# A layernorm's transposes take turns on the PSUM banks of the score maxima, not on those of heads and sums

## The chip, the cores and the metric

The kernel runs on one core of a Trainium2 chip. The metric is the device time of one execution in microseconds, from the first to the last instruction and what the launch adds around them; lower is better.

## What is computed

Eight sequences of 512 rows of 512 floats go through two layers: a cross attention to 77 rows of context (here "L", for L0) and then a block with self attention, a second cross attention (here "cross") and an MLP. Each begins with a layernorm. Cut to what matters:

```python
def cross_attention(x, context):                  # once as "L", once as "cross"
    h = layernorm(x)                              # "L" also scales and shifts it
    q = h @ Wq + bq                               # 16 heads of 32
    k, v = split(layernorm(context) @ Wkv + bkv)  # 77 keys, prepared ahead
    p = softmax(q @ k.T / sqrt(32))               # 512 x 77 for each head
    return x + (p @ v) @ Wp + bp
x = cross_attention(x, ctx)        # "L"
x = x + gate_a * self_attention(modulate(layernorm(x)))
x = cross_attention(x, ctx)        # "cross"
x = x + gate_m * mlp(modulate(layernorm(x)))
```

## The kernel before

Everything is float32 split into a high and a low part, so a product is three matmuls (`product`, line 396). Each engine has one instruction stream, written out in a fixed order by Python generators that `braid` interleaves step by step; between engines only semaphores order the work. A matmul's output goes to one of eight PSUM banks. A `Turns` ring hands its banks out in order, and `take` gives back what the bank's last user must have done before it may be written; TensorE (PE) waits for that.

A context attention works through 32 steps n: a batch b (of 8) and a group g of four heads (of 4). In a step PE has, interleaved:

- `attend`: four matmuls of scores by key (line 1318), banks 0 and 1, each read by ScalarE's exponential (line 1400). After the first of them `values` runs for the step before: the heads' sums over the values (line 1332, "heads") and the sums of the exponentials (line 1339, "sums"). These take the ring `pairs`, banks 6 and 7.
- `maxima` of step n + 3: for each of four tiles of rows, scores for the row maximum (line 396 on `key_diagonals`, M0 to M3 below), and VectorE's reduce (line 1217, `negated_max`). `max_rows` transposes the maxima (line 1304, R below), then ScalarE and VectorE write them in two parts (lines 1387 and 1225), and DMAs put them into the query stack. M0 to M3 and R take the ring `max_banks`, banks 2 and 3, in the order M0, R of the step before, M1, M2, M3.
- query products of a step further ahead and projections of the batch before (both line 396).

`Norm` normalises the rows of a coming batch and turns them: four groups of four transposes (line 354, T0 to T3 below), each into one bank. In "L" ScalarE modulates it into a float tile (line 377, which frees the bank) and splits it (379; VectorE 329). In "cross" ScalarE reads the bank for the high part (381) and VectorE reads it again for the low part (329), which frees it. The turns of batches 0 and 1 have a ring of their own. Those of batches 2 to 7 come in one step each, so there are six such places in each of the two attentions; a place begins with T0, in a step with g = 3, and ends in the next step, called ' below (M0', R', M1'). In "L" each is followed by a product of the modulation that belongs to the preparation (line 765), which takes a bank of `pairs` too:

```python
self.scores, self.max_banks, self.pairs = k.ring(0, 1), k.ring(2, 3), k.ring(6, 7)
```

```python
bk, before = self.ring(b).take((self, i), self.wide(i) if self.mods else self.lo(i))
if before:
    pe.wait_ge(*before)
for t in range(NT):
    turn = e.transpose(...)
```

Of the kernel before, what the change touches and what calls it, by code (L numbers as in the profile page):

```python
# [55 lines left out]
class Done:  # L56


    def __init__(self, sem, base, by):
        self.sem, self.base, self.by = sem, base, by  # L60
# [859 lines left out]
class CrossAttention:  # L920
# [5 lines left out]
    def __init__(self, k, w, name, layer, tail, first_banks, first_turns, x_in, x_ready, x_out, eps, mods, mods_ready, wq, bq, wp, bp, at):  # L926
        self.k, self.w, self.name, self.layer, self.tail = k, w, name, layer, tail
        self.x_in, self.x_out, self.wq, self.bq, self.wp, self.bp, self.at = x_in, x_out, wq, bq, wp, bp, at
        self.products, self.first_products = k.ring(4, 5), k.ring(*first_banks)
        self.scores, self.max_banks, self.pairs = k.ring(0, 1), k.ring(2, 3), k.ring(6, 7)  # L930
        self.norm = Norm(k, x_in, x_ready, eps, mods, mods_ready, 1, (k.ring(*first_turns), self.pairs), 2)
        n, c = LAST, k.count
        self.bias_loaded = c("dma_projection_bias", 1, 16)
        self.key_ones, self.diagonal_zeros = c("vector_key_ones", 2), c("pool_diagonal_zeros", 2)
        self.k_loaded, self.v_loaded = k.slots("key_stack", 2, B, 3), k.slots("values", 2, B)
        self.d_loaded = k.slots("key_diagonals", 2, B, 2 * GH)
        self.q_product = c("tensor_queries", n)
        self.q_hi, self.q_lo = c("scalar_queries_hi", n), c("vector_queries_lo", n)
        self.q_stored, self.q_stacked = k.slots("query_store", 2, n), k.slots("query_stack", 4, n, 3)
        self.smax, self.negmax = c("tensor_scores_for_max", n * NT), c("vector_negated_maxima", n * NT)  # L940
        self.rows_turned = c("tensor_turned_maxima", n)
        self.row_hi, self.row_lo = c("scalar_max_row_hi", n), c("vector_max_row_lo", n)
        self.rows_put = k.slots("max_rows", 4, n, 2)
        self.score, self.exp = c("tensor_scores_by_key", n * GH), c("scalar_exponentials", n * GH)
        self.av, self.summed = c("tensor_value_sums", n), c("tensor_exponential_sums", n)
        self.heads_copied, self.heads_hi = c("scalar_heads_float32", n), c("scalar_heads_hi", n)
        self.sums_turned, self.inverted = c("vector_sums_turned", n), c("vector_reciprocals", n)
        self.spread, self.normalised = c("vector_reciprocals_spread", n), c("vector_normalised_heads", n)
        self.heads_lo = c("vector_heads_lo", n)
        self.x_loaded, self.x_stored = k.slots("context_x_rows", 2, B), k.slots("context_x_out", 2, B)  # L950
        self.based, self.projected = c("pool_residual_bases", B * NT), c("tensor_projections", B * NT)
        self.added = c("vector_residuals", B * NT)
        self.place()
# [1425 lines left out]
```

## Time and profile before

| | |
|---|---|
| median of 3 runs | 2582.3 us (2569.95 to 2584.04) |
| profiled execution | 2574.66 us, span 2572.9 us |
| PE busy | 2401.8 us, 93% of the span |
| VectorE (DVE) busy | 1380.0 us, 54% |
| ScalarE (ACT) busy | 1026.1 us, 40% |
| mean granted TensorE clock | 0.972 |

The profiled execution is the one whose rows are read below. Its span is the time from its first to its last instruction; 1.8 us lie around it. The granted clock is a share of full speed: 1.00 is 2.4 GHz, 0.50 is 1.2 GHz.

### The profile page before, as it was taken

How to read it: one execution, taken by the hardware profiler on the slowest of the kernel's cores; microseconds unless marked ns; L12 is line 12 of the kernel's file. 1: busy time of each engine (PE TensorE's matmuls, PEld its weight loads, DVE VectorE, ACT ScalarE, POOL GpSimd, SP SyncE). 2: the span in 40 equal slices, each digit the busy share in tenths (PEclk: the TensorE clock that was granted, in tenths of full speed). 3: DMA queues.
4: the chain of work that ended last, by engine and by line, in shares of the span. 5: the costliest groups of instructions: out<-in, count | busy, mean ns of one | idle time of the engine just before them, and what ended most of it. 6: DMA issues, size and time to landing. Idle time of an engine off the chain costs nothing. (4 is left out here: it accounts for less than half of the span.)

```text
span 2572.9 us, 32327 instructions
## 1 busy us (share of the span) xinstructions
PE 2401.8 (93%) x12048; PEld 1683.8 (65%) x12048; DVE 1380.0 (54%) x2463; ACT 1026.1 (40%) x1831; POOL 588.1 (23%) x325
## 2 busy tenths in 40 slices
PE   6889999999979899999998789999899999999998
PEld 5656666678867344444444456766588888888887
DVE  4566666644546877776777456676743222222221
ACT  3454444423322455555554334444442322233231
POOL 2101111110000466665665411111211011101100
PEclk9899999999989899999999899999999999999999
DMA  6687777554564446565453568786531101110110
GB/s 205 193 216 229 206 216 200 173 197 176 180 212 147 104 112 153 132 153 130 116 144 90 146 157 221 200 230 184 166 114 58 58 1 58 58 58 1 58 42 17
DMA packets 261275, 354.19 MB, mean 138 GB/s; under 512 B 60979, under 2 KB 109195, under 8 KB 261118
## 3 DMA queue, kind: packets, MB, share of 16 engines
q1 hardware_dynamic: 259950, 348.27, 47.9%
q0 software_dynamic: 1168, 3.85, 0.4%
q8 instruction: 96, 1.57, 0.3%
q14 instruction: 61, 0.50, 0.1%
HBM read 233.78 MB, written 116.69 MB: 136 GB/s over the span
## 5 line engine op out<-in xcount | busy, mean ns | idle before, releaser
L1813 DVE TENSOR_REDUCE negated_max<-banks 128x1 f32<-128x512 f32 x512 | 331.8, 675 | 140.7 <-PE banks L1878 140.4
L1977 ACT ACTIVATE self_exponentials<-banks 128x512 f32<-128x512 f32 x512 | 286.3, 594 | 283.8 <-PE banks L1899 133.0
L1779 POOL TENSOR_TENSOR self_exponentials<-self_exponentials,self_exponentials 128x2048 f32<-128x2048 f32 x64 | 303.1, 4736 | 217.0 <-ACT self_exponentials L1977 217.0
L2177 PE MATMUL banks<-mlp_w_down_hi,out_parts 128*128 128x512 f32 x1024 | 333.8, 389 | 0.1
L337 POOL TENSOR_SCALAR norm_rstd<-norm_mean_var 128x4 f32<-128x4 f32 x32 | 8.0, 249 | 1336.3 <-DVE norm_mean_var L316 1336.3
L2134 DVE TENSOR_TENSOR out_parts<-wide,out_parts 128x512 fp32r<-128x512 f32 x128 | 93.1, 727 | 371.6 <-ACT out_parts L2206 371.6
L1899 PE MATMUL banks<-self_query_stack,self_key_stack 98*128 98x512 f32 x512 | 236.4, 463 | 26.3 <-ACT self_exponentials L1977 23.5
L2196 ACT ACTIVATE wide<-banks,bias_columns 128x512 f32<-128x512 f32 x128 | 88.3, 690 | 426.0 <-PE banks L396 425.9
L1899 PEld LDWEIGHTS banks<-self_query_stack,self_key_stack 98*128 98x128 f32 x512 | 98.1, 192 | 212.6 <-ACT self_exponentials L1977 173.3
L2177 PEld LDWEIGHTS banks<-mlp_w_down_hi,out_parts 128*128 128x128 f32 x1024 | 192.2, 188 | 40.4 <-DVE cross_last_x_rows L1261 0.5
L1878 PE MATMUL banks<-self_key_stack,self_query_stack 96*128 96x512 f32 x512 | 207.4, 408 | 2.3 <-DVE negated_max L1813 2.1
L2177 PE MATMUL banks<-mlp_w_down_lo,out_parts 128*128 128x512 f32 x512 | 199.2, 389 | 0.0
L1217 DVE TENSOR_REDUCE negated_max<-banks 128x4 f32<-128x308 f32 x256 | 121.0, 473 | 100.4 <-PE banks L396 96.7
L1921 PE MATMUL banks<-self_exponentials,self_values 128*32 128x512 f32 x1024 | 140.4, 621 | 0.7 <-ACT self_exponentials L1977 0.7
L312 DVE BATCH_NORM_STATS2 norm_stats<-norm_x 128x6 f32<-128x512 f32 x128 | 84.6, 671 | 67.0 <-DMA norm_x<-x 66.7
L1400 ACT ACTIVATE cross_exponentials<-banks 77x512 f32<-77x512 f32 x128 | 75.3, 591 | 106.6 <-PE banks L1318 106.6
L377 ACT ACTIVATE wide<-banks,modulation_columns 128x512 f32<-128x512 f32 x96 | 74.5, 776 | 104.7 <-PE banks L354 97.3
L396 PE MATMUL banks<-x_hi,w_qkv_hi 128*128 128x512 f32 x256 | 101.2, 395 | 16.0 <-DVE out_parts L1531 15.1
L1590 ACT ACTIVATE out_parts<-banks,bias_columns 128x512 fp32r<-128x512 f32 x64 | 44.1, 689 | 179.6 <-PE banks L396 144.1
L1400 ACT ACTIVATE L_exponentials<-banks 77x512 f32<-77x512 f32 x128 | 75.3, 591 | 87.9 <-PE banks L1318 87.7
L2177 PEld LDWEIGHTS banks<-mlp_w_down_lo,out_parts 128*128 128x128 f32 x512 | 96.1, 188 | 20.0
L1878 PEld LDWEIGHTS banks<-self_key_stack,self_query_stack 96*128 96x128 f32 x512 | 99.8, 195 | 14.2 <-DVE negated_max L1813 5.6
(208 smaller groups left out, 5253.4 us busy)
## 6 DMA issues: line engine op xcount, KB each, us to landing
L_query_stack<-q_parts_L SPq DMA_DIRECT2D x96, 256.0 KB, 4.8
norm_x<-x SPq DMA_DIRECT2D x24, 1024.0 KB, 7.5
self_query_stack<-q_parts_self SPq DMA_DIRECT2D x96, 256.0 KB, 4.0
self_key_stack<-k_parts_self SPq DMA_DIRECT2D x96, 256.0 KB, 6.3
cross_query_stack<-q_parts_cross SPq DMA_DIRECT2D x96, 256.0 KB, 5.0
x_rows<-x SPq DMA_DIRECT2D x23, 1024.0 KB, 6.7
x<-x_rows SPq DMA_DIRECT2D x22, 1024.0 KB, 5.0
q_parts_L<-out_parts SPq DMA_DIRECT2D x32, 512.0 KB, 4.6
```

What stands on the lines that cost most here:

```text
L396: mm = e.matmul(out_ap, l, r, start=i == 0, stop=i == len(terms) - 1)
L1217: e.tensor_reduce(k.nm[n % 2][:, t:GH * NT:NT], k.bank[:, bk, 0:GH * S].rearrange("p (h k) -> p h k", k=S), AX_X, ALU.max, negate=True).th ...
L1400: e.activation(self.p[:, i % self.HEADS_KEPT, :], k.bank[0:S, self.scores.of["score", i], :], ACT.Exp, scale=SCALE).then_inc(self.exp.sem, 1)
L1779: e.tensor_tensor(self.p[kt - 1][:], self.p[kt - 1][:], self.p[kt][:], ALU.add).then_inc(self.paired.sem, 1)
L1813: e.tensor_reduce(k.nm[n % 2][:, h * NT + t:h * NT + t + 1], k.bank[:, self.max_banks.of["max", i], :], AX_X, ALU.max, negate=True).then_i ...
L1878: e.matmul(k.bank[:, bk, :], self.q[n % 4][0:ST, h, t * P:(t + 1) * P], self.keys[n % 4][0:ST, h, :], start=True, stop=True).then_inc(self ...
L1899: e.matmul(k.bank[:, bk, :], self.keys[n % 4][0:ST_MAX, h, kt * P:(kt + 1) * P], self.q[n % 4][0:ST_MAX, h, :], start=True, stop=True).the ...
L1921: mm = e.matmul(k.bank[h * HD:(h + 1) * HD, bk, :], self.v[n % 3][:, kt, h * HD:(h + 1) * HD], self.p[kt][:, h, :], start=kt == 0, stop=kt ...
L1977: e.activation(self.p[kt][:, h, :], k.bank[:, self.scores.of["score", i], :], ACT.Exp, scale=SCALE).then_inc(self.exp.sem, 1)
L2134: e.tensor_tensor(h[:, 1, :], k.wides[k.wide_turns.of["up", i]][:], raw(h[:, 0, :]), ALU.subtract).then_inc(self.lo.sem, 1)
L2177: mm = e.matmul(bank, l, w, start=j == 0 and q == 0, stop=j == JC - 1 and q == 2)
L2196: e.activation(k.wides[w][:], k.bank[:, self.banks.of["up", i], :], ACT.Gelu_apprx_tanh, bias=k.bias_cols[:, col:col + 1]).then_inc(self.w ...
```

## The change

From batch 2 on, T0 to T3 of both context attentions take turns on banks 2 and 3 (`max_banks`) in place of banks 6 and 7 (`pairs`). No instruction is added, removed or moved on any engine. Only the banks change, and with them what PE waits for before it writes one.

```diff
         self.scores, self.max_banks, self.pairs = k.ring(0, 1), k.ring(2, 3), k.ring(6, 7)
-        self.norm = Norm(k, x_in, x_ready, eps, mods, mods_ready, 1, (k.ring(*first_turns), self.pairs), 2)
+        self.norm = Norm(k, x_in, x_ready, eps, mods, mods_ready, 1, (k.ring(*first_turns), self.max_banks), 2)
```

PE's stream in "cross", at the end of a place of a batch from 3 on. The first rows are T2 and T3, then come the first score of the next step, M0', R', the heads and the sums. In brackets stand the semaphores that a row waits for; `vector_norm_lo` is VectorE's low part, the last reader of a turned bank.

```order
+L354 MATMUL banks<-identity,norm_x 128x128 [waits vector_negated_maxima]
+L354 MATMUL banks<-identity,norm_x 128x128 x3
 L354 MATMUL banks<-identity,norm_x 128x128 [waits vector_norm_lo]
 L354 MATMUL banks<-identity,norm_x 128x128 x3
-L354 MATMUL banks<-identity,norm_x 128x128 [waits vector_norm_lo]
-L354 MATMUL banks<-identity,norm_x 128x128 x3
 L1318 MATMUL banks<-cross_query_stack_167,cross_key_stack_172 77x512 [waits dma_key_stack1,scalar_exponentials,dma_max_rows0,dma_query_stack0]
-L396 MATMUL banks<-cross_key_diagonals_174,out_parts_65 128x308 [waits vector_negated_maxima]
+L396 MATMUL banks<-cross_key_diagonals_174,out_parts_65 128x308 [waits vector_norm_lo]
 L396 MATMUL banks<-cross_key_diagonals_174,out_parts_65 128x308 x2
-L1304 MATMUL banks<-identity,negated_max_83 16x128 [waits vector_negated_maxima]
-L1332 MATMUL banks<-cross_exponentials,cross_values_175 32x512 [waits scalar_exponentials,vector_norm_lo]
```

The wait for T2's reader moved from the heads (line 1332) to M0', and the wait for T3's reader, which the sums (line 1339) had, moved to R' (line 1304), ahead of the heads and the sums. T2 itself now waits for the reduce of M3.

PE's stream in "L", the same place's end; `scalar_norm_float32` is ScalarE's modulation, the reader that frees a turned bank there.

```order
-L1304 MATMUL banks<-identity,negated_max_83 16x128 [waits vector_negated_maxima]
-L1332 MATMUL banks<-L_exponentials,L_values_130 32x512 [waits scalar_exponentials,scalar_norm_float32]
+L1304 MATMUL banks<-identity,negated_max_83 16x128 [waits scalar_norm_float32]
+L1332 MATMUL banks<-L_exponentials,L_values_130 32x512 [waits scalar_exponentials,scalar_heads_float32]
 L1332 MATMUL banks<-L_exponentials,L_values_130 32x512 x3
-L1339 MATMUL banks<-L_exponentials,ones 32x512 [waits scalar_norm_float32]
+L1339 MATMUL banks<-L_exponentials,ones 32x512 [waits vector_sums_turned]
 L1339 MATMUL banks<-L_exponentials,ones 32x512 x3
```

Here too the waits for ScalarE moved from the heads and sums to the two matmul groups ahead of them.

PE's stream in "cross" at the first of the six places (batch 2), where no projection stands between T0 and T3.

```order
-L354 MATMUL banks<-identity,norm_x 128x128 [waits scalar_heads_float32,vector_normed_rows]
+L354 MATMUL banks<-identity,norm_x 128x128 [waits vector_negated_maxima,vector_normed_rows]
 L354 MATMUL banks<-identity,norm_x 128x128 x3
 L1318 MATMUL banks<-cross_query_stack_170,cross_key_stack_171 77x512 [waits scalar_exponentials]
 L396 MATMUL banks<-cross_key_diagonals_174,out_parts_64 128x308 [waits vector_negated_maxima]
 L396 MATMUL banks<-cross_key_diagonals_174,out_parts_64 128x308 x2
-L354 MATMUL banks<-identity,norm_x 128x128 [waits vector_sums_turned]
-L354 MATMUL banks<-identity,norm_x 128x128 x3
 L354 MATMUL banks<-identity,norm_x 128x128 [waits vector_norm_lo]
```

T0 now waits for the reduce of M1, and T1 for T0's own reader, where it waited for the sums' transpose.

## Rows read from the trace of the kernel before

**Rows 1.** The page's head: span, and busy time by engine.

```profile
span 2572.9 us, 32327 instructions
...
PE 2401.8 (93%) x12048; PEld 1683.8 (65%) x12048; DVE 1380.0 (54%) x2463; ACT 1026.1 (40%) x1831; POOL 588.1 (23%) x325
```

**Rows 2.** Timeline, a later place of cross: start, us, engine, line, [idle before <-releaser].

```profile
1673.31 0.48 PE L1318 MATMUL banks<-cross_query_stack,cross_key_stack 98*77 98x512 f32 x1
...
1673.63 0.59 PE L396 MATMUL banks<-cross_key_diagonals,out_parts 128*128 128x308 f32 x3
...
1674.05 0.27 PE L1304 MATMUL banks<-identity,negated_max 128*16 128x128 f32 x1
...
1674.66 1.06 PE L1332 MATMUL banks<-cross_exponentials,cross_values 77*32 77x512 f32 x8 [0.34 <-DVE x_lo L329]
...
1675.93 1.06 PE L1339 MATMUL banks<-cross_exponentials,ones 77*32 77x512 f32 x8 [0.21 <-DVE x_lo L329]
1676.39 0.47 DVE L1217 TENSOR_REDUCE negated_max<-banks 128x4 f32<-128x308 f32 x1
...
1676.93 0.46 PE L1318 MATMUL banks<-cross_query_stack,cross_key_stack 98*77 98x512 f32 x1
1677.22 0.59 PE L396 MATMUL banks<-cross_key_diagonals,out_parts 128*128 128x308 f32 x3
```

**Rows 3.** Timeline, the next step of cross, where nothing holds the heads.

```profile
1683.46 0.69 PE L396 MATMUL banks<-cross_key_diagonals,out_parts 128*128 128x308 f32 x3 [0.63 <-DVE out_parts L1203]
...
1683.99 0.27 PE L1304 MATMUL banks<-identity,negated_max 128*16 128x128 f32 x1
...
1685.08 1.04 PE L1339 MATMUL banks<-cross_exponentials,ones 77*32 77x512 f32 x8
```

**Rows 4.** Timeline, a later place of L.

```profile
278.46 1.07 PE L1339 MATMUL banks<-L_exponentials,ones 77*32 77x512 f32 x8 [0.74 <-ACT wide L377]
...
279.46 0.45 PE L1318 MATMUL banks<-L_query_stack,L_key_stack 98*77 98x512 f32 x1
...
280.44 0.57 ACT L1413 COPY heads_float<-banks 128x512 f32<-128x512 f32 x1
...
280.83 0.69 PE L396 MATMUL banks<-L_key_diagonals,out_parts 128*128 128x308 f32 x3 [0.92 <-DVE negated_max L1217]
...
281.45 1.08 PE L765 MATMUL banks<-prepare_mod_weights_late,repare_silu_cond_columns 128*32 128x128 f32 x32
```

**Rows 5.** Timeline, the first place of cross (batch 2).

```profile
1535.60 0.63 PE L354 MATMUL banks<-identity,norm_x 128*128 128x128 f32 x4
1535.68 0.47 DVE L1217 TENSOR_REDUCE negated_max<-banks 128x4 f32<-128x308 f32 x1
...
1536.27 0.60 ACT L381 ACTIVATE x_hi<-banks 128x512 fp32r<-128x512 f32 x1 [0.32 <-PE banks L354]
...
1537.21 0.63 DVE L329 TENSOR_TENSOR x_lo<-banks,x_hi 128x512 fp32r<-128x512 f32 x1
...
1539.47 0.66 PE L354 MATMUL banks<-identity,norm_x 128*128 128x128 f32 x4 [0.92 <-DVE x_lo L329]
```

**Rows 6.** Windows of 15 us from T0: length, busy by engine, PEclk, DMA.

```profile
270.00:285.00 15.00, 13.34 (x107) 9.53 (x106) 9.99 (x22) 10.43 (x18) 0.00 (x0) 1.00 0.88 231
318.00:333.00 15.00, 13.34 (x95) 9.14 (x94) 8.42 (x17) 9.60 (x17) 0.00 (x0) 0.82 0.91 248
368.00:383.00 15.00, 13.34 (x100) 9.32 (x99) 8.55 (x17) 9.73 (x17) 0.00 (x0) 0.89 0.92 242
...
1668.00:1683.00 15.00, 14.29 (x84) 10.33 (x82) 11.56 (x23) 7.94 (x15) 0.00 (x0) 1.00 0.96 256
```

**Rows 7.** Timeline of PE: T0 of three places of L that follow each other.

```profile
270.61 0.60 PE L354 MATMUL banks<-identity,norm_x 128*128 128x128 f32 x4
...
317.91 0.60 PE L354 MATMUL banks<-identity,norm_x 128*128 128x128 f32 x4
...
368.04 0.60 PE L354 MATMUL banks<-identity,norm_x 128*128 128x128 f32 x4
```

## The prediction, made before the changed kernel ran

> **What bounds the kernel now.** I read the page's head first: PE is busy for 2401.8 of 2572.9 us [rows 1], so nearly every microsecond that PE is made to wait lengthens the run, unless a later wait of PE shrinks by as much. Then I read the timeline at the places where the layernorm's rows are turned, since the change touches nothing else. There are 6 in "L" and 6 in "cross". Last came the windows with the granted clock around these places.
>
> At a later place of "cross" (five are alike, to 0.01 us in the two waits) the reader is to see this [rows 2]. After the first score of the next step at 1673.31, M0' runs at 1673.63 and R' at 1674.05 without a wait. The heads wait 0.34 us for VectorE's low part of T2 and start at 1674.66. The sums wait 0.21 us for the low part of T3 and start at 1675.93. The second score follows at 1676.93 and M1' at 1677.22. So the waits for T2 and T3 are mostly covered: M0', R' and the heads run while VectorE works on T2 and T3.
>
> In "L" the sums start at 278.46 after a wait of 0.74 us for ScalarE, and M1' at 280.83 after another of 0.92 us, for VectorE's reduce of M0' [rows 4].
>
> **The change, part by part.** It adds and removes no instruction. It moves waits on PE, and PE's order is fixed, so what stands behind a wait is held with it.
>
> *The end of a later place in "cross".* M0' takes T2's bank and waits for T2's reader, which the heads row gives: 1674.66. R' takes T3's bank and waits for T3's reader: 1675.93, the time at which the sums started before. Behind R' now stand the heads and the sums. In the next step, where nothing holds them, the sums start 1685.08 - 1683.99 = 1.09 us after R' [rows 3], and from the sums to the second score it is 1676.93 - 1675.93 = 1.00 us [rows 2]. So the second score comes at 1675.93 + 1.09 + 1.00 = 1678.02 in place of 1676.93: 1.09 us later. Does a later wait give it back? VectorE's reduce of M0' at 1676.39 stands in its stream behind the low part of T3, which is no later than before, so it stays there, and M1' needs it only at 1678.3. From the second score on PE has no wait until 1683.46, and that one, 0.63 us, is for the query's low part [rows 3], which follows PE's own product and moves with it. The work on T3 is not delayed, and the DMAs that follow R' start with a reduce and a copy that stand behind T3's on their engines anyway. So the 1.09 us stay: 5 x 1.09 = 5.5 us.
>
> *The end of a later place in "L".* R' waits for ScalarE's modulation of T3, until 278.46; the second score comes 1.09 + 1.00 us behind it, at 280.55 in place of 279.46. But M1' waited until 280.83 for the reduce anyway, so the 0.92 us of that wait cover most of it, and M1' starts at about 280.85. What is late next is ScalarE's copy of the heads: it began 0.98 us after the second score, at 280.44, and now begins at 280.55 + 0.98 = 281.53, and ends 0.57 us later at 282.10. The modulation's product (line 765) takes the heads' bank. It started at 281.45 and now starts at 282.1 to 282.15: 0.7 us later [rows 4]. With PE full behind it, that stays: 5 x 0.7 = 3.5 us.
>
> *The first place of each (batch 2).* No projections stand between T0 and T3 there. In "cross" T0 started at 1535.60; now it waits for the reduce of M1, which ends at 1535.68 + 0.47 = 1536.15, so it starts at 1536.2. T1 then waits for T0's low part: 0.67 us to the high part, 0.60 for it, 0.03 and 0.63 to 0.69 for the low part, so 1538.2. T1 has the same chain in front of T3, some 2.0 us, so T3 starts at 1540.2 in place of 1539.47: 0.7 us later [rows 5]. The end of the place adds its 1.09 us: 1.8 us. In "L" T0 waits for the same reduce, and I take the same 0.7 us plus that place's 0.7 us: 1.4 us. Bounds for these two together: 1.8 us (no delay of the start) to 5 us (the delay of T0 and that of T1 add up). I take 3.2 us.
>
> *The other new waits* cost nothing while their reduces end in time. T0 of the later places waits for the reduce of M1, T1 for T0's reader (which T2 needed before anyway) and T2 for the reduce of M3; in the timeline each of these has ended before PE is there. If that cover were gone, it would cost up to the reduce's 0.47 us a place, 5 us in all for ten places.
>
> *Sum without the clock:* 5.5 + 3.5 + 3.2 = 12.2 us.
>
> *The clock.* Three of the six places of "L" ran at full clock, as the first row of [rows 6] does, and three did not: a granted clock of 0.82 at two and of 0.89 at one, which is a stretch at 1.2 GHz behind the waits of 0.74 and 0.92 us. All six of "cross" had 1.00. From T0 to T0 it is 47.30 us without such a stretch and 50.13 us with one [rows 7], so the dip between them cost 2.8 us. The windows say the same: (1 - 0.82) x 15 us = 2.7 us, and (1 - 0.89) x 15 us = 1.6 us for the shorter one. After the change PE stands idle in "cross" from the end of the first score, 1673.31 + 0.48 = 1673.79, to 1674.66, and from the end of M0', 0.59 us later at 1675.25, to 1675.93: 0.87 + 0.68 = 1.55 us within 2.2 us, close to the 0.74 + 0.92 = 1.66 us that dipped in half of the cases in "L". So I take three dips at 1.6 us in "cross", 4.8 us, and leave those of "L" as they are, since there one wait grows while the other goes. Bounds: 0, and six dips of 2.8 us, 17 us.
>
> The Trainium skill (TensorE: Matmul & The Clock Gate, "A second HAM failure mode: psum-queue depth-cycling") says that short idles of PE between groups of matmuls, from cycling through PSUM banks, can make the clock swing between its two levels. The trace agrees in "L" and not in "cross". By that rule the sum would be 12.2 us and the dips on top, without it 12.2 us alone.
>
> *Result.* 12.2 + 4.8 = 17.0 us on top of the profiled execution's 2574.66 us gives 2591.7. That execution lies 7.6 us below the median of the runs shown, 2582.3; from the median it would be 2599.3. The runs shown scatter by 14 us, so I take the middle, 2595 us.
>
> **The rivals.**
>
> *The delay is absorbed (same).* If the heads and sums, once late, only push into waits that PE has later, as the 0.92 us in "L" do, "cross" would lose nothing more than its first place, and "L" little: 12.2 - 5.5 = 6.7 us or less, and no dips. Against it: PE has only the one wait of 0.63 us in the 6.5 us after, and that moves along. The same end is reached if all goes as I say but no dip comes: 12.2 us is 0.47%. Time: 2575 to 2594 from the two bases, middle 2585.
>
> *The clock dips at most places.* For it: the idle time stands closer together than it did in "L". Then 12.2 us and 9 dips more at 1.6 to 2.8 us: 27 to 37 us, a time of 2602 to 2620, middle 2611. Against it: three places of "L" with the same waits had none.
>
> *It gets faster.* The mechanism: the waits of heads and sums go (0.34 + 0.21 us in "cross", 0.74 in "L" [rows 2, 4]) and nothing takes their place, because T2 and T3 are read early enough for M0' and R'. That would give 5 x 0.55 + 6 x 0.74 = 7.2 us, and with the idle time the three dips of "L" could go (2.8 + 2.8 + 1.6 us): 14 us less, 2560 to 2568. It decides at whether T3's reader has ended when PE is ready for R' at 1674.05. It would have to end 1.9 us earlier than it does, and its own chain is not shortened.
>
> *The change doesn't do what it says* is no case: the order of the streams shows the banks moved.
>
> **How the numbers follow.** My forecast (12 us and a few dips) 0.5, absorbed or without dips 0.32, many dips 0.12, faster 0.06. The range takes in the first two and the lower part of the third: 2582 to 2609. A measurement of this kernel can tell about 0.5%, 12.9 us, from no change. Of my forecast's 0.5, 0.45 lies above that; with the many dips and a little of the second case slower comes to 0.6, same 0.35, faster 0.05.
>
> **What would show it.** In the profile after, at later places of "cross": R' with a wait of about 0.7 us for VectorE's low part, heads and sums without one, the second score 1.1 us later against T0. In "L": a wait of over 1 us at R', M1' no later against T0 than before, line 765 behind the heads' copy. The distance from T0 to T0 in "cross" should grow by 1.1 us, by more where a window shows a clock below 1.00. I am wrong if the second score in "cross" is not later, if a reduce holds T0 or T2, or if the clock falls at places without such waits.

## The result, and the profile after

The changed kernel is slower: 2599.54 us, median of 8 runs (2589.53 to 2608.16), against 2578.72 us for the kernel before (8 runs, 2569.95 to 2586.18). The ratio is 1.0078, 95% interval 1.005 to 1.0107, some 20 us. The profiled execution took 2602.08 us with a span of 2600.3 us, 27.4 us more than the profiled one before. Both kernels scatter by 16 to 19 us from run to run, so two single profiles don't give the difference of the medians; where it comes from is read in the timeline at the places.

A later place of "cross", timeline of the changed kernel; compare [rows 2].

```profile
1686.62 0.60 PE L354 MATMUL banks<-identity,norm_x 128*128 128x128 f32 x4
...
1691.70 0.48 PE L1318 MATMUL banks<-cross_query_stack,cross_key_stack 98*77 98x512 f32 x1
...
1693.06 0.69 PE L396 MATMUL banks<-cross_key_diagonals,out_parts 128*128 128x308 f32 x3 [0.87 <-DVE x_lo L329]
...
1693.59 0.69 DVE L329 TENSOR_TENSOR x_lo<-banks,x_hi 128x512 fp32r<-128x512 f32 x1 [0.58 <-ACT x_hi L381]
...
1694.33 0.28 PE L1304 MATMUL banks<-identity,negated_max 128*16 128x128 f32 x1 [0.58 <-DVE x_lo L329]
1694.54 1.07 PE L1332 MATMUL banks<-cross_exponentials,cross_values 77*32 77x512 f32 x8
...
1695.42 1.04 PE L1339 MATMUL banks<-cross_exponentials,ones 77*32 77x512 f32 x8
...
1696.39 0.46 PE L1318 MATMUL banks<-cross_query_stack,cross_key_stack 98*77 98x512 f32 x1
1696.69 0.59 PE L396 MATMUL banks<-cross_key_diagonals,out_parts 128*128 128x308 f32 x3
```

M0' now waits 0.87 us and R' 0.58 us, both for VectorE's low parts (line 329), and the heads and sums follow without a wait of their own. From the first score to the second it is 1696.39 - 1691.70 = 4.69 us; before it was 1676.93 - 1673.31 = 3.62 us [rows 2]: 1.07 us more.

A later place of "L" in the changed kernel; compare [rows 4].

```profile
378.48 0.69 PE L396 MATMUL banks<-L_key_diagonals,out_parts 128*128 128x308 f32 x3 [0.20 <-ACT wide L377]
...
380.56 0.28 PE L1304 MATMUL banks<-identity,negated_max 128*16 128x128 f32 x1 [1.40 <-ACT wide L377]
...
382.62 0.46 PE L1318 MATMUL banks<-L_query_stack,L_key_stack 98*77 98x512 f32 x1
382.93 0.69 PE L396 MATMUL banks<-L_key_diagonals,out_parts 128*128 128x308 f32 x3
...
383.61 0.57 ACT L1413 COPY heads_float<-banks 128x512 f32<-128x512 f32 x1
...
384.24 1.08 PE L765 MATMUL banks<-prepare_mod_weights_late,repare_silu_cond_columns 128*32 128x128 f32 x32 [0.62 <-ACT heads_float L1413]
```

The wait of 1.40 us stands at R'. M1' (382.93) has none left and is no later against T0 than before: 382.93 - 372.70 = 10.23 us, where it was 280.83 - 270.61 = 10.22 us [rows 4, 7]. The product of line 765 waits 0.62 us for ScalarE's copy of the heads and starts 11.54 us after T0, where it was 10.84 us: 0.70 us later.

T0 of later places in the changed kernel, PE's timeline: two of "L" and three of "cross".

```profile
372.70 0.60 PE L354 MATMUL banks<-identity,norm_x 128*128 128x128 f32 x4
...
420.66 0.60 PE L354 MATMUL banks<-identity,norm_x 128*128 128x128 f32 x4
...
1637.72 0.60 PE L354 MATMUL banks<-identity,norm_x 128*128 128x128 f32 x4
...
1732.35 0.60 PE L354 MATMUL banks<-identity,norm_x 128*128 128x128 f32 x4
...
1778.08 0.60 PE L354 MATMUL banks<-identity,norm_x 128*128 128x128 f32 x4
```

With T0 at 1686.62 from above, the distances in "cross" are 48.90, 45.73 and 45.73 us, where the kernel before had 44.64 to 44.71. In "L" 47.96 us stands against 47.30 [rows 7]. So a place costs 1.08 us more in "cross" and 0.66 us more in "L", and one distance of "cross" has 3.17 us on top. The windows with the granted clock around the six places of "cross" say why (length, PE busy, PEclk, DMA):

```profile
1544.00:1559.00 15.00, 12.42 (x56) 0.77 1.06 246
1591.00:1606.00 15.00, 13.55 (x82) 1.00 0.90 235
1637.00:1652.00 15.00, 13.54 (x69) 0.82 0.92 244
1686.00:1701.00 15.00, 13.54 (x82) 1.00 0.94 245
1732.00:1747.00 15.00, 13.55 (x82) 1.00 0.93 254
1778.00:1793.00 15.00, 13.54 (x67) 0.79 0.97 232
```

Three of the six places have a stretch at 1.2 GHz now, a "dip" in what follows; in the kernel before the clock was 1.00 at all six, one of which stands in [rows 6]. The window that begins at 1637 is the distance of 48.90 us. Windows of 1 us there show the fall, behind a wait of 0.88 us at M0' and one of 0.57 us at R', which ends at 1645.46:

```profile
1645.00:1646.00 1.00, 0.54 (x5) 1.00 1.06 358
1646.00:1647.00 1.00, 1.00 (x12) 0.84 0.94 209
1647.00:1648.00 1.00, 1.00 (x8) 0.50 1.08 259
```

At the first place of "cross" T0 waits for the reduce of M1, T1 and T3 for VectorE's low parts, M0' and R' too:

```profile
1544.18 0.63 PE L354 MATMUL banks<-identity,norm_x 128*128 128x128 f32 x4 [0.74 <-DVE negated_max L1217]
...
1546.23 1.09 PE L354 MATMUL banks<-identity,norm_x 128*128 128x128 f32 x8 [0.46 <-DVE x_lo L329]
...
1548.30 0.66 PE L354 MATMUL banks<-identity,norm_x 128*128 128x128 f32 x4 [0.98 <-DVE x_lo L329]
...
1550.77 0.28 PE L1304 MATMUL banks<-identity,negated_max 128*16 128x128 f32 x1 [0.51 <-DVE x_lo L329]
```

The reduce of M1 began at 1543.57 here and at 1535.68 before [rows 5]. Against it T3 (1548.30) is 0.94 us later and T0 0.69 us; I had 0.7 for T3.

The first place of "L" has a wait that I had not named. T0 waits 0.78 us for the reduce of M1, as expected, and T2 waits for a reduce as well:

```profile
178.54 1.09 PE L354 MATMUL banks<-identity,norm_x 128*128 128x128 f32 x8 [1.11 <-DVE negated_max L1217]
```

Against the reduce of M1 (it began at 177.34 before and at 174.66 now) the product of line 765 still starts only 1.40 us later, at 10.93 in place of 9.53 us.

### The profile page after: what moved, and what is told of

Its sections match the earlier page's. It is cut to its first block and busy times, and to the rows that moved or that the text cites. A ratio compares the mean times of both kernels' runs of the same rounds, so it can differ in the third digit from the quotient of the medians.

```text
span 2600.3 us, 32327 instructions
## 1 busy us (share of the span) xinstructions
PE 2417.1 (93%) x12048; PEld 1686.7 (65%) x12048; DVE 1380.5 (53%) x2463; ACT 1028.3 (40%) x1831; POOL 588.8 (23%) x325
## 5 line engine op out<-in xcount | busy, mean ns | idle before, releaser
L396 PE MATMUL banks<-x_hi,w_qkv_hi 128*128 128x512 f32 x256 | 100.8, 394 | 17.3 <-DVE out_parts L1531 16.4
```

Of the source, the lines that this page charges most:

```text
L396: mm = e.matmul(out_ap, l, r, start=i == 0, stop=i == len(terms) - 1)
```

## The experiments

My theory: 12 us of the loss are waits that moved in front of the heads and sums, and the rest is the clock, which falls because PE now stands idle at the places of "cross". The rivals: the turns' own new waits for the reduces cost the time; or the clock falls elsewhere and by chance. Each time is a median of 12 runs (7 for only "cross"), against 17 to 35 runs of the kernel before on the same chip. The ratio is taken from all the runs and differs from the quotient of the two medians by up to 0.0012.

| kernel | us | before, us | ratio, 95% interval |
|---|---|---|---|
| only "L" changed | 2586.38 | 2582.21 | 1.0009 (0.9993 to 1.0025) |
| only "cross" changed | 2594.67 | 2582.21 | 1.0049 (1.0027 to 1.0071) |
| T0, T1 changed, T2, T3 not | 2585.91 | 2582.21 | 1.0007 (0.9992 to 1.0023) |
| T3 on a bank of the products | 2580.56 | 2582.21 | 1.0000 (0.9984 to 1.0016) |
| changed kernel, waits filled | 2583.69 | 2579.85 | 1.0020 (1.0006 to 1.0034) |
| kernel before, waits of "L" filled | 2571.25 | 2579.85 | 0.9971 (0.9958 to 0.9985) |
| T3 on the products, heads first | 2573.15 | 2579.85 | 0.9978 (0.9964 to 0.9991) |
| changed kernel, heads first | 2573.51 | 2579.85 | 0.9987 (0.9970 to 1.0003) |
| T3 on the products, heads first, "L" filled | 2568.73 | 2579.07 | 0.9964 (0.9946 to 0.9983) |

### One attention at a time

```diff
-        self.norm = Norm(..., (k.ring(*first_turns), self.max_banks), 2)
+        self.norm = Norm(..., (k.ring(*first_turns), self.max_banks if name == "L0" else self.pairs), 2)
```

and the same with `name == "cross"`.

Expected of "L" alone: 

> Only "L" turns its rows on the banks of the maxima; "cross" is as before. My theory (waits moved ahead of the heads and sums): the distance from T0 to T0 in L is 47.97 us where the clock is full, and that of cross 44.65; the waits cost 5 x 0.67 + 1.4 = 4.8 us, and the time is 4 to 8 us above before, ratio 1.0015 to 1.003. Rival (the extra time of the changed kernel comes from somewhere else, as the clock between the stages): the ratio stays near 1.008 or falls to 1.000 whatever the distances say.

Expected of "cross" alone: 

> Only "cross" turns its rows on the banks of the maxima; "L" is as before. My theory: T0 to T0 in cross 45.73 us at full clock, in L 47.30; the waits cost 5 x 1.08 + 2.0 = 7.4 us and a few stretches at the lower clock come on top, where before had none; 9 to 16 us above before, ratio 1.004 to 1.006. Rival (stretches at the lower clock fall anywhere, the places have nothing to do with them): 7 us, 1.003, and all places of cross at clock 1.00.

Measured: 1.0009 and 1.0049, together 1.0058, which the interval of the full change holds. Windows of the kernel with only "cross" changed, at its places of "cross" (the first and the third of six):

```profile
1540.00:1555.00 15.00, 12.08 (x56) 0.77 1.12 261
...
1633.00:1648.00 15.00, 13.54 (x68) 0.81 0.91 242
```

and of the one with only "L" changed, at the third place of "cross":

```profile
1635.00:1650.00 15.00, 14.45 (x86) 1.00 0.92 249
```

The dips in "cross" come and go with the change there: three of six places with it (the first, the third and the last, as in the changed kernel), none of six without. Without it T0 to T0 is 44.67 us there. In "L" the expected ratio of 1.0015 to 1.003 was missed on the low side, though the interval holds it. Its profile showed a clock below 1.00 at all six places of "L".

### Only the first two turns moved

```diff
-            bk, before = self.ring(b).take((self, i), ...)
+            bk, before = self.ring(b, c).take((self, i), ...)
...
+(k.ring(*first_turns), (self.max_banks, self.max_banks, self.pairs, self.pairs))
```

> In both attentions T0 and T1 of the batches from 2 on take the banks of the maxima, T2 and T3 those of heads and sums as before. This keeps the new waits of T0 and T1 and takes away those of M0' and R' for T2 and T3. My theory: the later places are as before (44.65 and 47.30 us from T0 to T0), only the first place of each is 0.7 to 0.9 us longer; 0 to 3 us, ratio 1.000 to 1.001. Rival (the waits of the turns for the reduces are what costs): most of the 20 us remain, ratio above 1.004.

Measured: 1.0007. All windows of the later places of "cross" have the clock at 1.00, and the first has 0.89. Two of its T0s in "cross", and the windows of the first and the last place of "L":

```profile
1625.86 0.60 PE L354 MATMUL banks<-identity,norm_x 128*128 128x128 f32 x4
...
1670.57 0.60 PE L354 MATMUL banks<-identity,norm_x 128*128 128x128 f32 x4
```

```profile
177.00:192.00 15.00, 12.03 (x85) 0.78 0.97 234
...
422.00:437.00 15.00, 13.34 (x108) 1.00 0.87 219
```

44.71 us is the kernel before. So at the later places the turns' own waits for the reduces are not what costs, and the rival falls. At the first place of "cross" they do cost: T0 waits 0.73 us for the reduce there, the heads 0.92 us for a low part, a dip follows, and it is 45.09 us to the next T0 where the kernel before had 43.27. The windows of "L" show something else: with the waits of the kernel before at the later places, five of the six places had a clock below 1.00 in this run, and five again in the run of only "cross", which leaves "L" as it was. The three of six in the profile that I predicted from were few.

### Are the waits on PE what lowers the clock?

Matmuls whose result nobody reads are put into the waits (the bank is written again by the next score). The only intended difference to the changed kernel, or to the kernel before, is that PE works there:

```diff
+        def fill(times):
+            bk = self.scores.banks[self.scores.given % 2]
+            pe.wait_ge(*self.scores.free[bk])
+            for _ in range(times):
+                e.matmul(k.bank[:, bk, :], qh[:, 0, 0:P], qh[:, 0, :], start=True, stop=True)
```

On the changed kernel: 

> The changed kernel with matmuls that compute nothing needed in the new waits: in cross three ahead of M0' and two ahead of R' at the six places, in L five ahead of R'; each some 0.23 us, into the scores' bank that is free just then. My theory (12 us of moved waits, the rest is the clock that falls because PE stands idle at the places): T0 to T0 in cross 45.7 to 45.9 us at all five distances with no stretch at the lower clock, and fewer of them in L; the ratio to before falls from 1.008 to 1.002 to 1.005. Rival (the clock falls by chance or for another reason): stretches at the lower clock as often as in the changed kernel, ratio 1.008 or more.

On the kernel before: 

> The kernel before with three such matmuls ahead of the sums and three ahead of M1' at the six places of L. My theory: the stretches at the lower clock at the places of L, five or six of which stood in other runs, go or get rarer, T0 to T0 in L 47.3 to 47.4 us; 4 to 10 us less than before, ratio 0.996 to 0.9985. Rival: the clock is not set by these waits, and the ratio is 1.000 to 1.001.

Measured: 1.0020 and 0.9971. The windows of all twelve places are at 1.00 in the first, and of all six of "L" in the second. A place of the first, and its T0s (the added lines move the numbers: 1277 is the fill, 1329 the scores, 1315 is R'):

```profile
1586.37 0.48 PE L1329 MATMUL banks<-cross_query_stack,cross_key_stack 98*77 98x512 f32 x1
1586.69 0.87 PE L1277 MATMUL banks<-cross_w_q_hi 128*128 128x512 f32 x3
1587.72 0.69 PE L396 MATMUL banks<-cross_key_diagonals,out_parts 128*128 128x308 f32 x3 [0.16 <-DVE x_lo L329]
1588.25 0.63 PE L1277 MATMUL banks<-cross_w_q_hi 128*128 128x512 f32 x2
1588.99 0.28 PE L1315 MATMUL banks<-identity,negated_max 128*16 128x128 f32 x1
...
1591.05 0.46 PE L1329 MATMUL banks<-cross_query_stack,cross_key_stack 98*77 98x512 f32 x1
```

```profile
1581.28 0.60 PE L354 MATMUL banks<-identity,norm_x 128*128 128x128 f32 x4
...
1627.00 0.60 PE L354 MATMUL banks<-identity,norm_x 128*128 128x128 f32 x4
...
1672.73 0.60 PE L354 MATMUL banks<-identity,norm_x 128*128 128x128 f32 x4
```

From score to score it is 4.68 us, as in the changed kernel, and T0 to T0 is 45.72 and 45.73 us: the fill gives nothing back of what the moved waits cost and adds nothing to it. It takes away the dips. Filled, the kernel before has

```profile
267.40 0.60 PE L354 MATMUL banks<-identity,norm_x 128*128 128x128 f32 x4
...
314.66 0.60 PE L354 MATMUL banks<-identity,norm_x 128*128 128x128 f32 x4
```

47.26 us, with no dip in any distance. The two filled kernels differ in the moved waits and in where the fill stands (five matmuls at each of the twelve places in one, six at the six of "L" in the other): 1.0020 / 0.9971 = 1.0049, 12.7 us, where I had summed 12.2. The slowest of the 12 runs of one, 2577.09 us, is faster than the fastest of the other, 2580.68.

The two terms can also be told apart over all runs, since each has its span and mean granted clock. As an estimate, span x (1 - clock) is what a run lost to the lower clock, and span x clock is the rest. It overstates the loss a little: PE's waits inside a dip count too. Means, in us; their standard errors go up to 1.7 at full clock and to 3.3 in what is lost:

| kernel (runs) | at full clock | lost to the clock |
|---|---|---|
| before (30; 35) | 2502.5; 2501.4 | 77.7; 76.5 |
| changed (8) | 2511.4 | 85.7 |
| only "L" changed (12) | 2504.1 | 78.6 |
| only "cross" changed (7) | 2507.0 | 86.3 |
| changed, filled (12) | 2515.3 | 67.6 |
| before, "L" filled (12) | 2504.2 | 65.8 |

The changed kernel has 9 to 10 us more of the first and 8 to 9 us more of the second. With only "L" changed the clock takes no more than before (0.9 us, within the error), with only "cross" changed it takes 8.6 us more, and in the filled kernels that excess is gone.

### Is it what is queued behind R'?

```diff
                 e.matmul(...)                     # the score by key of head h
-                yield
                 if h == 0 and n > 0:
                     values(n - 1)                 # heads and sums
+                yield                             # M0 and R get their turn here
```

On the changed kernel: 

> The changed kernel with that order: heads and sums ahead of M0' and R', so nothing but the second score is queued behind R's wait for T3's reader. My theory (the loss at a later place is what stands queued behind R'): the second score comes 0.7 us earlier than in the kernel before, against T0, and T0 to T0 in cross is 44.3 to 44.8 us, not 45.73; ratio 0.998 to 1.002. Rival (the wait itself costs, or the maxima that come late do): 45.7 us or more, ratio 1.006 or more.

Its timeline at a later place, with the T0s of that place and the next:

```profile
1665.46 0.60 PE L354 MATMUL banks<-identity,norm_x 128*128 128x128 f32 x4
...
1670.55 0.48 PE L1318 MATMUL banks<-cross_query_stack,cross_key_stack 98*77 98x512 f32 x1
...
1670.96 1.06 PE L1332 MATMUL banks<-cross_exponentials,cross_values 77*32 77x512 f32 x8
...
1673.35 0.27 PE L1304 MATMUL banks<-identity,negated_max 128*16 128x128 f32 x1
1673.37 0.48 PE L1318 MATMUL banks<-cross_query_stack,cross_key_stack 98*77 98x512 f32 x1
...
1674.16 0.69 PE L396 MATMUL banks<-cross_key_diagonals,out_parts 128*128 128x308 f32 x3 [0.31 <-DVE negated_max L1217]
...
1709.14 0.60 PE L354 MATMUL banks<-identity,norm_x 128*128 128x128 f32 x4
```

Measured: 0.9987, and 43.68 us from T0 to T0, a better distance than I had allowed (44.3 to 44.8). With the same banks and the same semaphores waited for as in the changed kernel the loss of 1.08 us is gone, because the heads and sums, now ahead of M0' and R', cover the waits for the readers of T2 and T3: neither M0' nor R' has one. From score to score it is 2.82 us. Of the 0.97 us below the kernel before, 0.3 is this place and the rest is the wait of 0.63 us for the query's low part one step later [rows 3], which heads and sums cover as well; that part I had left out. The same order with the banks of the kernel before was not run; the nearest to it is the next section's version with T3 on a bank of the products.

### Versions meant to beat both kernels

T3 alone on a bank of the products: 

> As before, but T3 takes a bank of the products (4 or 5), so the heads wait for T1's reader and the sums for T2's, and nothing on PE waits for T3's but a query product some 4 us later. If the waits of heads and sums for T2 and T3 still cost something in the kernel before: in cross the second score comes 0.8 us earlier, but M1' then waits for the reduce of M0', so 0.3 us of it is left, T0 to T0 44.35 us; in L M1' waits for the reduce anyway, so 47.30 us as before; 1 to 3 us less, ratio 0.999 to 1.000. Rival (the idle time that is now in one piece at M1' lowers the clock more often): slower by 2 to 6 us.

```diff
+(k.ring(*first_turns), (self.pairs, self.pairs, self.pairs, self.products))
```

Measured: no difference, 1.0000. T0 to T0 in "cross" is 44.5 us in its profile, 0.15 us a place, below what a time can show. With it and the heads first: 

> The kernel with T3 on a bank of the products, and PE's heads and sums directly behind the first score of each step of both attentions, ahead of M0 and R. Theory: the wait of 0.63 us for the query's low part ahead of M0 is then covered by heads and sums in the steps that have it, and at the places the second score comes earlier; 4 to 10 us less than before, ratio 0.996 to 0.9985. Rival: the reduces and R come 1.9 us later in each step, VectorE's stream waits for them, and M1 waits for the reduce of M0: slower by 5 us or more.

Measured: 0.9978, as expected. In its profile five of the six places of "L" still had a dip, behind a wait of 1.8 us at M1', here at one of them:

```profile
278.12 0.69 PE L396 MATMUL banks<-L_key_diagonals,out_parts 128*128 128x308 f32 x3 [1.85 <-DVE negated_max L1217]
```

Over its 12 runs it has 12 us less than the kernel before at full clock (2489.4) and 5 us more lost to the clock (81.9). So seven matmuls were put ahead of M1' too: 

> T3 on a bank of the products, heads and sums directly behind the first score of each step, and seven matmuls that compute nothing needed ahead of M1' at the six places of L, where PE waits 1.8 us. If moved waits and the clock are separate terms, they add: T0 to T0 in cross 43.8 us, in L 46.5 to 46.6 us at all five distances with no stretch at the lower clock; 9 to 15 us less than the kernel before, ratio 0.994 to 0.9965. Rival: matmuls in front of the wait delay M1' or keep the clock no better, and the ratio stays at 0.998.

Measured: 0.9964, 0.9946 to 0.9983, 10 us below the kernel before and 2568.73 us in all; the rival's 0.998 is still inside the interval, but the profile bears out the dips' part. In its timeline T0 to T0 is 46.98 us in "L" and 43.77 us in "cross", with no dip at the places. 46.98 is 0.4 us above what I expected: the fill waits for an exponential itself (0.62 us at one place), and M1' has no wait left behind it, so the fill ends after the reduce and delays M1'. Fewer matmuls may do there; that was not run.

## Why the prediction was right, step by step

It said slower, 2595 us in a range of 2582 to 2609, and the time is 2599.54. The middle of its two bases, 2578.5 us, happened to be what the 8 runs of the kernel before gave (2578.72), though only 3 were known; so the 4 us or so that are missing are the terms' and not the base's.

- *The end of a later place in "cross"*, 1.09 us each: 1.07 from score to score and 1.08 from T0 to T0. Right; the heads-first kernel shows that it goes when heads and sums stand ahead of the waits. R' waited 0.58 us and not 0.68, since M0' took 0.69 us behind its wait and not 0.59; the release came when expected.
- *The end of a later place in "L"*, 0.7 us each, from ScalarE's copy of the heads after M1's wait had swallowed the rest: 0.70 us at line 765 and 0.66 from T0 to T0, with the 0.62 us of wait where it was expected.
- *The first places*, 3.2 us for both. In "cross" T3 was 0.94 us later and not 0.7: the low part of T0 took 0.69 us where I reckoned with 0.63 to 0.69, and PE came to each transpose a little after its release. So this term was slightly small: 0.94 + 1.1 = 2.0 us in place of 1.8. In "L" it was the 1.4 us I took, but not all by my path: besides T0, the reduce held T2 for 1.11 us, which I had not foreseen.
- *The sum without the clock*, 12.2 us: the two filled kernels put it at 12.7, the estimate over all runs at 9 to 10.
- *The clock*, 4.8 us. The mechanism was right, the size too small. Three dips came at the six places of "cross", as I had taken them, but I had priced each at 1.6 us, the smallest of the three in "L", without a reason to pass over the two of 2.7 to 2.8 us. One cost 3.17 us by its distance, and the three windows, at 0.77, 0.82 and 0.79, make (1 - clock) x 15 us = 3.5, 2.7 and 3.2 us; two of these windows end inside their dip, and in windows of 1 us each of the three comes to 3.4 us. That is 9.4 to 10.2 us in this profile, and 8 to 9 us over all runs. With the 12.2 us it makes 20 to 22, against 20.8 between the medians. That it was three was partly luck: I took it from half of the places in "L", where five of six dipped in two other runs.
- *"L" left as it is.* The filled kernel before is 0.29% faster, so the dips in "L" were already paid before: 7.5 us. The changed kernel's profile had a clock below 1.00 at two of its six places, the kernel before's at three, and windows of 1 us give 8.5 us in both. Over the runs of only "L" changed the clock took 0.9 us more, within the error.
- *The absorbed rival* (0.32) would have had "cross" lose only its first place. No wait behind took the 1.08 us back. *The reduces* that might hold the turns cost nothing at later places, as said.

The Trainium skill's rule (TensorE: Matmul & The Clock Gate, "A second HAM failure mode: psum-queue depth-cycling") held here at some of the places: the clock swung between its two levels behind short idles of PE between groups of matmuls, at three of six in "cross", and the filled kernels show that it was these idles. The first place of "cross" dipped with only T0 and T1 changed too.

The 27.4 us between the two profiles divide in the same way: by their clocks of 0.972 and 0.966 the kernel before lost 72.0 us and the changed one 88.4, 16.4 us more, and 11.0 us are at full clock. Of the 16.4 the three dips at places of "cross" are 10.2. Another 5.1 is a dip from 1837 to 1849, after the last place, which begins as a wait of R of 1.77 us for a reduce ends; the kernel with only "L" changed lost 6.8 us there, so the change in "cross" is not needed for it. What stays open is why some places dip and others with the same waits don't.

## What to carry to other kernels

A ring of PSUM banks is also a list of what waits for whom: moving a tile to another ring moves its reader's wait to that ring's next writer, so look up which matmul that is and how much work is queued behind it on PE. A wait is cheapest behind the longest work that does not need it; here moving one line in the order took back all that the change of banks had cost, and the choice of bank for T3 alone was worth nothing that a time could show. And where PE idles twice in a row for a good half microsecond or more, price the lower clock behind it too, or fill the idle with matmuls that nobody reads.

## What the runs showed of the hardware

Behind two idles of PE of 0.87 and 0.58 us, one matmul group apart and with PE busy before and behind, the granted clock fell from 2.4 to 1.2 GHz at two of the five later places of "cross", in one profile of each of two kernels. Behind 0.34 and 0.21 us it stayed up at all five. In "L", behind 0.74 and 0.92 us, it fell at three of the five later places in one profile and at four in each of two others. With two to five matmuls of 128x512 in each wait of the changed kernel it stayed up at all twelve places. One such stretch cost 3.17 us, about three times the 1.08 us that the moved waits cost a place by themselves.
